# Cross attention, self-attention and mixture of experts on one core: where the self-attention weights are dequantised, and in what order the v projection stands

## Chip, cores, metric

The kernel runs on one core of one Trainium2 chip. The metric is the device time of one execution in microseconds (us), the median of several runs. A profiled execution gives a trace; its span runs from the first to the last instruction.

## What is computed

Three blocks, each added to its input: a cross attention of 128 query rows over 12544 context rows, a self-attention over the 128 rows, and a routed feed-forward block of 32 experts with one shared block. Cut to what matters here:

```
x = x + cross_attention(layernorm(x), context)       # 16 heads of 32; 257 image rows and 12287 text rows apart
x = x + self_attention(layernorm(x))                 # 16 heads of 128
x = x + moe(layernorm(x))

def mxfp4_matmul(x, codes, scales, block_size=32):
    w = codes * repeat(scales, block_size, axis=0)
    return x @ w
# in self_attention, D = 512, feat = 2048
q = mxfp4_matmul(x, wq_codes, wq_scales) + bq        # codes 512x2048, scales 16x2048; k and v alike
attn = softmax(q k^T / sqrt(128))
return mxfp4_matmul(attn v, wo_codes, wo_scales) + bo    # codes 2048x512, scales 64x512
```

Codes and scales are float32. One scale holds for 32 rows of codes, so a tile of 128 rows of codes takes 4 rows of scales, each repeated over 32 partitions. Multiplying codes by repeated scales is called dequantising below.

## The kernel before

The program is written engine by engine: each engine has its own instruction list in the order of the code, and semaphores (the names that begin with e_) say what an instruction waits for. SP issues every DMA, all on one queue. Nothing is scheduled by a planner.

**The key loop.** The context is worked through in 25 groups of 512 keys (NG = 25), each in 4 tiles of 128 (GT = 4). `steps` runs steps s = 0 to 26; step s projects group s (k and v), takes the scores and the softmax of group s - 1, and finishes group s - 2. A step goes over 16 heads; in each, TensorE does one product of queries with the stacked keys (L947), six products of a projection (L916), four transposes of softmax rows (L908) and, every fourth head, the 32 products with v (L1011). VectorE takes the row maximum (L730), folds it into the running maximum with a one-column operation between SBUF tensors (L732), and copies the transposed rows (L739). ScalarE takes the exponential (L559). GpSimd splits each context tile into a high and a low part (L470 `cx_hi`, L473 `cx_lo`) and makes the norm factors of the keys (L449, L451). SP loads the next group (L305) and builds `k_stack` for the next step in two halves of 12 DMAs of 128 KB each, SBUF to SBUF (L333); the second half waits for the last `kt_lo` (L766). The first product of the next step waits for both halves. Step 25 has no projection, step 26 only finishes.

**From the key loop to the self-attention.** After step 26 the outputs are divided, projected with `wo` (L1035) and added to x (L785, this is x1); then comes a layer norm, whose last operation is L666 (`yn`).

**The self-attention before.** The codes of q, v, k and o are loaded whole (4 MB each, `load_codes`), and their scales by sixteen 1 MB items into a ring of three buffers (`load_scales`, L361, 4 DMAs an item). `dequantise` (L285) multiplies 128x2048 elements of codes by one item, in place: the four of q and the first two of v on GpSimd behind its key loop, the other ten on VectorE between other work. TensorE projects q, v, then k (L1052, 16 products of 128x512 each), transposes the heads of q between v and k and those of k behind k (L908), takes the scores (L1073), transposes the softmax (L908), multiplies by v (L1085) and projects with the codes of o (L1090, 16 products). An item is loaded only when the buffer that it takes has been used up (`ring_free`).

**The experts.** 34 expert slices of 1.5 MB each follow through 8 slots; the first eight are released by the projections of the self-attention (`e_pj`).

## Time and profile before

| | |
|---|---|
| median of 3 runs (lowest, highest) | 1351.44 us (1350.98, 1356.18) |
| time of the profiled execution | 1353.21 us |
| its span | 1351.4 us |
| TensorE busy | 1258.6 us (93%) |
| VectorE busy | 997.9 us (74%) |
| ScalarE, GpSimd busy | 716.8 us (53%), 342.8 us (25%) |
| mean granted TensorE clock | 0.972 |

The profiled execution's time is 1.8 us over its span and 1.8 us over the median. A row of the timeline gives start, duration (both in us from the span's start; of several merged instructions the time from the first start to the last end), engine, line, operation, output<-inputs, how many, and in brackets the idle time before it with what ended it.

### The profile page before, as it was taken

The numbers are of one execution on the slowest core, as the hardware profiler recorded it, in microseconds if no ns is written. First come the engines' busy times: TensorE is split into PE (matmuls) and PEld (weight loads), VectorE is DVE, ScalarE is ACT, GpSimd is POOL, SyncE is SP. The second block draws the span as 40 slices with busy tenths as digits, with TensorE's granted clock in tenths as the row PEclk, the third lists the DMA queues.
The fourth block names the chain that finished last, engine by engine and source line by source line (L and its number), as shares of the span: only waits on it lengthen the run. The fifth ranks groups of instructions, "written<-read, shape, count | busy, mean of one in ns | idle before, by whom it ended". The sixth has DMA issues, their size and how long they took to land.

```text
span 1351.4 us, 26518 instructions
## 1 busy us (share of the span) xinstructions
PE 1258.6 (93%) x9046; PEld 998.6 (74%) x9046; DVE 997.9 (74%) x1761; ACT 716.8 (53%) x1580; POOL 342.8 (25%) x435
## 2 busy tenths in 40 slices
PE   5799999999999999999999999999998576789998
PEld 3588888888888888888888888888886332568886
DVE  3667777777777777777777777777778733659998
ACT  3646555555555555555555555555554100447776
POOL 4433222333222333222332222332221430000000
PEclk9899999999999999999999999999999687889999
DMA  7554333554333454333444333444339999969991
GB/s 272 125 157 95 95 99 89 124 124 93 91 100 89 124 124 93 88 100 92 124 124 93 85 100 94 124 120 97 83 69 268 272 271 279 312 236 368 368 358 58
DMA packets 128181, 205.34 MB, mean 152 GB/s; under 512 B 12688, under 2 KB 90512, under 8 KB 124688
## 3 DMA queue, kind: packets, MB, share of 16 engines
q1 hardware_dynamic: 128144, 204.86, 53.8%
q8 instruction: 21, 0.34, 0.1%
q14 instruction: 16, 0.13, 0.0%
HBM read 125.91 MB, written 0.26 MB: 93 GB/s over the span
## 4 chain that ended last, share of the span: by engine, by line
PE 56%; DVE 14%; issue 12%; ACT 7%; POOL 5%; DMA 4%; SPq 1%; ACTq 0%; DVEq 0%; POOLq 0%
PE ps L916 24%; PE ps L908 9%; PE ps L947 5%; DVE small L730 5%; PE ps L1011 5%; DMA scale_ring<-wk_scales 3%; ACT kt_hi L572 3%; POOL small L451 2%; DVE kb L746 2%; PE ps L1113 2%; PE ps L1116 2%; PE ps L1119 2%; DVE small L732 2%; DMA scale_ring<-wo_scales 1%; PE ps L1134 1%
## 5 line engine op out<-in xcount | busy, mean ns | idle before, releaser
L559 ACT ACTIVATE p<-ps,small 128x512 f32<-128x512 f32 (+2 forms) x400 | 271.8, 679 | 387.0 <-DVE small L732 376.7
L739 DVE COPY pt<-ps 128x512 f32<-128x512 f32 x400 | 276.0, 690 | 96.5 <-PE ps L908 95.2
L730 DVE TENSOR_REDUCE small<-ps 128x1 f32<-128x512 f32 (+2 forms) x400 | 268.3, 671 | 16.2 <-PE ps L947 16.1
L908 PE MATMUL ps<-ident,p 128*128 128x128 f32 x1600 | 241.3, 273 | 6.9 <-ACT p L559 6.9
L908 PEld LDWEIGHTS ps<-ident,p 128*128 128x128 f32 x1600 | 199.9, 140 | 59.6 <-ACT p L559 7.6
L947 PE MATMUL ps<-k_stack,q_stack 96*128 96x512 f32 x400 | 194.8, 488 | 18.3 <-ACT p L559 18.2
L470 POOL TENSOR_TENSOR cx_hi<-cx,small 128x512 fp32r<-128x512 f32 x100 | 104.6, 1046 | 215.7 <-PE ps L916 211.1
L916 PE MATMUL ps<-w_hi_k,cx_hi 128*128 128x512 f32 x384 | 151.8, 395 | 5.0 <-ACT v_sb L581 5.0
L766 DVE TENSOR_TENSOR kt_lo<-ps,kt_hi 128x512 fp32r<-128x512 f32 x100 | 69.2, 692 | 116.7 <-ACT kt_hi L572 116.7
L916 PE MATMUL ps<-w_lo_k,cx_hi 128*128 128x512 f32 x384 | 151.4, 394 | 0.0
L916 PE MATMUL ps<-w_hi_k,cx_lo 128*128 128x512 f32 x384 | 151.3, 394 | 0.0
L916 PE MATMUL ps<-w_hi_v,cx_lo 128*128 128x512 f32 x384 | 151.2, 394 | 0.0
L916 PE MATMUL ps<-w_hi_v,cx_hi 128*128 128x512 f32 x384 | 151.0, 393 | 0.0
L916 PE MATMUL ps<-w_lo_v,cx_hi 128*128 128x512 f32 x384 | 150.8, 393 | 0.0
L449 POOL TENSOR_TENSOR small<-small 128x1 f32<-128x1 f32 x100 | 19.2, 192 | 457.3 <-ACT squares L548 457.3
L473 POOL TENSOR_TENSOR cx_lo<-cx,cx_hi 128x512 fp32r<-128x512 f32 x100 | 130.9, 1309 | 7.8
L732 DVE TENSOR_TENSOR small<-small 128x1 f32<-128x1 f32 x400 | 117.5, 294 | 13.8
L947 PEld LDWEIGHTS ps<-k_stack,q_stack 96*128 96x128 f32 x400 | 76.0, 190 | 46.6 <-ACT p L559 27.4
L1011 PE MATMUL ps<-pt,v_sb 128*32 128x128 f32 x3200 | 108.9, 277 | 0.8 <-DVE pt L739 0.8
L1011 PEld LDWEIGHTS ps<-pt,v_sb 128*32 128x32 f32 x3200 | 81.8, 110 | 17.8 <-issue 16.5
L548 ACT ACTIVATE squares<-kb 128x512 f32<-128x512 f32 x100 | 63.1, 631 | 59.2 <-DVE kb L746 59.1
L829 DVE TENSOR_TENSOR w_lo<-expert,w_hi 128x2048 fp32r<-128x2048 f32 x34 | 77.8, 2292 | 10.5 <-ACT w_hi L622 10.5
(195 smaller groups left out, 1952.2 us busy)
## 6 DMA issues: line engine op xcount, KB each, us to landing
expert<-experts SPq DMA_DIRECT2D x34, 1536.0 KB, 8.9
k_stack<-kt_hi SPq DMA_DIRECT2D x400, 128.0 KB, 2.3
k_stack<-kt_lo SPq DMA_DIRECT2D x200, 128.0 KB, 2.3
cx<-ctx_t SPq DMA_DIRECT2D x24, 1024.0 KB, 5.0
codes_q<-wq_codes SPq DMA_DIRECT2D x2, 2048.0 KB, 13.6
scale_ring<-wq_scales SPq DMA_DIRECT2D x16, 256.0 KB, 20.7
codes_v<-wv_codes SPq DMA_DIRECT2D x1, 4096.0 KB, 37.6
scale_ring<-wv_scales SPq DMA_DIRECT2D x16, 256.0 KB, 14.1
```

Source lines behind the costliest of these rows:

```text
L470: eng.tensor_tensor(cx_hi[:, :, part], cx[:, :, part], one_col.unsqueeze(2).broadcast_to((P, DC, P)), ALU.mult).then_inc(e_chi, 1)
L473: eng.tensor_tensor(cx_lo[:, :, part], cx[:, :, part], cx_hi[:, :, part].bitcast(F32), ALU.subtract).then_inc(e_clo, 1)
L559: eng.activation(pb[:, lo:hi], ps_s[h % NS][:, lo:hi], exp, bias=nm[1 - par][:, h:h + 1], accum_out=ls[1 - par][:, h:h + 1]).then_inc(e_ex ...
L730: eng.tensor_reduce(ngm[:, h:h + 1], ps_s[h % NS][:, lo:hi], AX.X, ALU.max, negate=True).then_inc(e_gm, 1)
L732: eng.tensor_tensor(nm[1 - par][:, h:h + 1], ngm[:, h:h + 1], old[:, h:h + 1], ALU.min).then_inc(e_nm, 1)
L739: eng.tensor_copy(pt_sb[hp % NPT][:, :], ps_pt[hp % 2][:, :]).then_inc(e_pte, 1)
L766: eng.tensor_tensor(kt_lo[:, :, part], ps_t[:, :].rearrange("p (c k) -> p c k", c=DC), kt_hi[:, :, part].bitcast(F32), ALU.subtract).then_ ...
L829: eng.tensor_tensor(w13_lo[n % 2][:, :, :], slot[n % NR][:, 0:DC, :], w13_hi[n % 2][:, :, :].bitcast(F32), ALU.subtract).then_inc(e_13lo, 1)
L908: last = eng.transpose(dst[:, c * P:(c + 1) * P], src[:, c * P:(c + 1) * P], ident[:, :])
L916: last = eng.matmul(dst, *steps[k], start=(k == 0), stop=(k == len(steps) - 1))
L947: eng.matmul(ps_s[h % NS][:, :], q_st[qi][0:NST * HD, h, :], stk[1 - par][0:NST * HD, h, :], start=True, stop=True).then_inc(e_qk, 1)
L1011: last = eng.matmul(ps_o[jp * HD:(jp + 1) * HD, c * P:(c + 1) * P], vb[:, k, head * HD:(head + 1) * HD], pt_sb[head % NPT][:, k * P:(k + 1 ...
```

## The change

- Codes and scales are laid out on the host as 64 tiles of 128x512 (16 of each matrix). In steps 2 to 23 of the key loop, three tiles a step, SP loads a tile of codes (256 KB) and its scales (4 DMAs of 64 KB in SBUF) into one of two small buffers, GpSimd multiplies them (`scale_codes`, a 128x512 operation), and SP stores the product to a scratch tensor `scaled` in HBM (`pass_codes`).
- After the key loop the four matrices are loaded whole from `scaled` (`load_matrix`, 4 MB each). Nothing is dequantised behind the key loop any more, on GpSimd or VectorE. The q and k biases and `bo` are asked for at other places of the queue: `bo` directly behind the matrix o.
- The order of the projections is q, k, v. The transposes of q stand between the blocks of k; three of the four blocks of v stand behind the scores, among the transposes of the softmax. The product with o waits for each quarter of its input apart.
- VectorE adds the four v biases between the steps of its softmax, and adds `bo` to x1 before the first of them.
- Buffers are placed anew; `wo` is loaded behind the key loop instead of in step 1.

The diff, cut to its core (a line of ... marks what is left out):

```diff
-        QKV = "qvk"
-        codes = {n: sb(f"codes_{n}", off * KB, [P, DC, SF]) for n, off in (("q", 0), ("v", 64), ("k", 32))}
-        codes_o = sb("codes_o", 96 * KB, [P, SH, D])
-        NRING = 3
-        ring = [sb(f"scale_ring{i}", (144 + 8 * i) * KB, [P, SF]) for i in range(NRING)]
...
+        QKV = "qkv"
+        NWT = SH
+        NW = 4 * NWT
+        W_STEP, W_FIRST = 3, 2
+        codes = [sb(f"codes{i}", (96 + 4 * i) * KB, [P, D]) for i in range(2)]
+        code_scale = [sb(f"code_scale{i}", (98 + 4 * i) * KB, [P, D]) for i in range(2)]
...
-        def dequantise(eng, n, c, done):
-
-            eng.wait_ge(e_codes[n], 16 * (c // (DC // 2) + 1 if n == "q" else 1))
-            scale = ring_loaded(eng, scales(n, c))[:, :]
-            part = codes_o[:, c * HB:(c + 1) * HB, :] if n == "o" else codes[n][:, c, :]
-            if n == "o":
-                scale = scale.rearrange("p (c f) -> p c f", c=HB)
-            eng.tensor_tensor(part, part, scale, ALU.mult).then_inc(done, 1)
...
+        scaled = nc.dram_tensor("scaled", (NW, P, D), F32, kind="Internal").ap()
+
+        def tile_of(array, i):
+            return array[i:i + 1] if isinstance(i, int) else array[bass.ds(i, 1)]
...
@@ -315,12 +296,33 @@
             load_weight(2)
             load_weight(3)
 
+            def pass_codes(s, k, par, loop):
+
+                i = s * W_STEP + (k - W_FIRST * W_STEP)
+                if not loop and not 0 <= i <= NW:
+                    return
+                b = (par + k) % 2
+                if loop or i >= 1:
+                    eng.wait_ge(e_cm, i)
+                    eng.dma_start(tile_of(scaled, i - 1).rearrange("o p f -> p (o f)"), codes[1 - b][:, :]).then_inc(e_cs[1 - b], 16)
+                if not loop and i == NW:
+                    return
+                if loop or i >= 2:
+                    eng.wait_ge(e_cs[b], i * 8 - 8 * b)
+                eng.dma_start(codes[b][:, :], tile_of(t["codes"], i).rearrange("o p f -> p (o f)")).then_inc(e_cl[b], 16)
+                for r in range(P // QB):
+                    eng.dma_start(code_scale[b][r * QB:(r + 1) * QB, :],
+                                  tile_of(t["code_scales"], i)[:, r, :].partition_broadcast(QB)).then_inc(e_cl[b], 16)
+
...
                     eng.wait_ge(e_clo, s * GT + GT)
                     load(s + 1)
+                if not loop and s == W_FIRST:
+                    eng.wait_ge(e_qk, NH)
+                pass_codes(s, 0, par, loop)
                 if not loop and s == 1:
                     eng.wait_ge(e_vp, GT)
...
                         for j in range(HC):
                             eng.dma_start(stk[par][r * HD:(r + 1) * HD, j::HC, keys].bitcast(F32),
                                                      part[j * HD:(j + 1) * HD, :, keys].bitcast(F32)).then_inc(e_stk, 16)
-                if not loop and s == 1:
-                    eng.wait_ge(e_qk, NH)
-                    eng.dma_start(wo[:, :, :], wview(t["o_wt"])).then_inc(e_wo, 16)
+                    pass_codes(s, 1 + half, par, loop)
 
...
+            def load_matrix(n):
+
+                i = (QKV + "o").index(n) * NWT
+                eng.dma_start(weight[n][:, :, :], scaled[i:i + NWT].rearrange("i p f -> p i f")).then_inc(e_wl[n], 16)
 
...
-            eng.wait_ge(e_kp, NG * GT)
-            load_codes("q", 0)
-            eng.wait_ge(e_clo, NG * GT)
-            load_scales("q", 0)
+            for b in range(2):
+                eng.wait_ge(e_cs[b], 16 * (NW // 2))
+            eng.wait_ge(e_vp, NG * GT)
+            load_matrix("q")
+            eng.dma_start(wo[:, :, :], wview(t["o_wt"])).then_inc(e_wo, 16)
             eng.wait_ge(e_stk, (16 * HALVES * NST * HC) * NG)
             for i, n in enumerate(["o_b", "v_b", "v_img_b"]):
...
+            load_bias("q")
+            load_bias("k")
             eng.wait_ge(e_qk, (NG - 1) * NH)
-            load_codes("v")
-            load_scales("q", 3)
-            load_scales("v", 0)
-            load_scales("v", 1)
-            eng.wait_ge(e_pv, NG * NH // HC)
-            load_bias("q")
-            load_scales("v", 2)
-            load_scales("v", 3)
+            load_matrix("k")
+            eng.wait_ge(e_pv, (NG - 1) * (NH // HC))
             load_bias("v")
             eng.wait_ge(e_qk, NG * NH)
-            load_codes("k")
+            load_matrix("v")
             eng.wait_ge(e_x1, 1)
-            for c in range(DC):
-                load_scales("k", c)
-            load_bias("k")
-            load_codes("o")
-            for c in range(NB):
-                load_scales("o", c)
+            load_matrix("o")
...
@@ -449,6 +421,14 @@
                 eng.tensor_tensor(k_t[:, j:j + 1], k_ss[:, j:j + 1], rms_eps, ALU.add).then_inc(e_rt, 1)
                 eng.wait_ge(e_rt, s * GT + j + 1)
                 eng.tensor_tensor(k_r[:, j:j + 1], k_t[:, j:j + 1], minus_half, ALU.pow).then_inc(e_r, 1)
...
+            def scale_codes(i, b, loop):
+
+                if not loop and not 0 <= i < NW:
+                    return
+                n = 16 * (1 + P // QB)
+                eng.wait_ge(e_cl[b], i * (n // 2) + (n - b * n // 2))
+                eng.tensor_tensor(codes[b][:, :], codes[b][:, :], code_scale[b][:, :], ALU.mult).then_inc(e_cm, 1)
...
+                    if j % 2 == 1:
+                        k = (j + 1) // 2
+                        scale_codes(s * W_STEP + (k - (W_FIRST + 1) * W_STEP), (1 - par + k) % 2, loop)
...
+                scale_codes(s * W_STEP - W_FIRST * W_STEP, par, loop)
...
-            steps(eng, step)
-            for c in range(DC):
-                dequantise(eng, "q", c, e_deqp)
+            steps(eng, step, peeled=1)
             eng.wait_ge(e_var, 2)
             rsqrt(rstd, mv[:, 1:2], ln_eps)
-            for c in range(NPOOL - DC):
-                dequantise(eng, "v", c, e_deqp)
...
-            for b in range(NB):
-                add_bias("q", b)
-                if b < NB - 1 and NPOOL - DC + b < DC:
-                    dequantise(eng, "v", NPOOL - DC + b, e_deq)
-            for b in range(NB):
-                add_bias("v", b)
-                dequantise(eng, "k", b, e_deq)
-            for b in range(NB):
-                add_bias("k", b)
-            for c in range(NB // 2):
-                dequantise(eng, "o", c, e_deq)
+            for n in "qk":
+                for b in range(NB):
+                    add_bias(n, b)
+            eng.wait_ge(e_bo, 16)
+            chain(eng.tensor_tensor(x1[:, :], x1[:, :], bo_row[:, :], ALU.add))
+            add_bias("v", 0)
             for b in range(NB):
...
                 eng.tensor_scalar(s_nb[:, hs], s_max[:, hs], -SD ** -0.5, None, ALU.mult).then_inc(e_smax, 1)
             for b in range(NB):
+                if b < NB - 1:
+                    add_bias("v", b + 1)
...
-            for c in range(NB // 2, NB):
-                dequantise(eng, "o", c, e_deq)
-            eng.wait_ge(e_bo, 16)
-            chain(eng.tensor_tensor(x1[:, :], x1[:, :], bo_row[:, :], ALU.add))
...
-            project("q")
-            project("v")
-            transpose_heads("q", 0)
-            project("k")
-            transpose_heads("k", NB)
-            eng.wait_ge(e_trc, 2 * NB)
-            for b in range(NB):
...
+            def project(n, b):
+                i = QKV.index(n) * NB + b
+                if b == 0:
+                    eng.wait_ge(e_wl[n], 16)
+                if i >= 2:
+                    eng.wait_ge(e_pjb, i - 1)
+                for c in range(DC):
+                    last = eng.matmul(ps_pj[b % 2][:, :], ynt[:, c * P:(c + 1) * P], weight[n][:, c * NB + b, :],
+                                      start=(c == 0), stop=(c == DC - 1))
+                last.then_inc(e_pj, 1)
+
...
-            for b in range(NB + 1):
-                if b < NB:
-                    eng.wait_ge(e_sn, b + 1)
-                    if b >= 2:
...
+            def weigh_values(b):
+                eng.wait_ge(e_sptc, b + 1)
+                eng.wait_ge(e_pjb, 2 * NB + b + 1)
+                for h in range(b * HB, (b + 1) * HB):
+                    part = slice(h * P, (h + 1) * P)
+                    last = eng.matmul(ps_sc[b][:, (h % HB) * P:(h % HB + 1) * P], sv[:, part], spt[:, part], start=True, stop=True)
+                last.then_inc(e_so, 1)
...
+            for b in range(NB):
+                project("q", b)
+            for b in range(NB):
+                project("k", b)
+                transpose_heads("q", b)
+            for b in range(NB - 1):
+                transpose_heads("k", b)
+            project("v", 0)
+            transpose_heads("k", NB - 1)
+            for b in range(NB):
+                scores(b)
+            project("v", 1)
+            project("v", 2)
+            transpose_p(0)
+            project("v", 3)
+            transpose_p(1)
+            for b in range(NB):
+                weigh_values(b)
+                if b + 2 < NB:
+                    transpose_p(b + 2)
+            eng.wait_ge(e_wl["o"], 16)
             for h in range(SH):
-                last = eng.matmul(ps_pj[0][:, :], sot[:, h * P:(h + 1) * P], codes_o[:, h, :], start=(h == 0), stop=(h == SH - 1))
+                if h % HB == 0:
+                    eng.wait_ge(e_soc, h // HB + 1)
+                last = eng.matmul(ps_pj[0][:, :], sot[:, h * P:(h + 1) * P], weight["o"][:, h, :], start=(h == 0), stop=(h == SH - 1))
             last.then_inc(e_sf, 1)
```

Three places of the program follow, on SP, GpSimd and TensorE; the names in them are the tiles, with buffer numbers.

SP, step 2 of the key loop, between the two halves of `k_stack` (the later steps are alike, with register instructions for the addresses); before:

```order
L333 DMA k_stack_63<-kt_hi 32x4x256 x4
L333 DMA k_stack_63<-kt_hi 32x4x256 [waits kt_lo]
L333 DMA k_stack_63<-kt_hi 32x4x256 x3
L333 DMA k_stack_63<-kt_lo 32x4x256 x4
L333 DMA k_stack_63<-kt_hi 32x4x256 x4
```

and now:

```order
L335 DMA k_stack_63<-kt_hi 32x4x256 x4
L307 DMA scaled<-codes_104 128x512 [waits codes_scaled]
L312 DMA codes_105<-codes 128x512
L314 DMA code_scale_107<-code_scales 32x512 x4
L335 DMA k_stack_63<-kt_hi 32x4x256 [waits kt_lo]
L335 DMA k_stack_63<-kt_hi 32x4x256 x3
L335 DMA k_stack_63<-kt_lo 32x4x256 x4
```

Six DMAs now stand between the halves. Another six stand behind the second half, and six behind the load of the context.

GpSimd, in the loop, around the second context tile of a step; before:

```order
L470 TENSOR_TENSOR cx_hi<-cx,small 128x4x128 [waits v_projected]
L472 REGISTER_ALU
L473 TENSOR_TENSOR cx_lo<-cx,cx_hi 128x4x128 [waits cx_hi]
L469 REGISTER_ALU
L470 TENSOR_TENSOR cx_hi<-cx,small 128x4x128 [waits v_projected]
```

and now:

```order
L450 TENSOR_TENSOR cx_hi<-cx,small 128x4x128 [waits v_projected]
L452 REGISTER_ALU
L453 TENSOR_TENSOR cx_lo<-cx,cx_hi 128x4x128 [waits cx_hi]
L430 ISA
L431 TENSOR_TENSOR codes_105<-codes_105,code_scale_107 128x512 [waits codes_loaded1]
L449 REGISTER_ALU
L450 TENSOR_TENSOR cx_hi<-cx,small 128x4x128 [waits v_projected]
```

A multiplication of codes stands behind the second split; a second one stands behind the fourth, a third behind the last norm factor.

TensorE, self-attention, from the scores on; before:

```order
L1073 MATMUL ps<-skt,sqt 128x128 [waits self_transposed_stored]
L1073 MATMUL ps<-skt,sqt 128x128 x15
L908 MATMUL ps<-ident,sq 128x128 [waits self_normed]
L908 MATMUL ps<-ident,sq 128x128 x3
L908 MATMUL ps<-ident,sq 128x128 [waits self_normed]
L908 MATMUL ps<-ident,sq 128x128 x3
L1085 MATMUL ps<-sk,sv 128x128 [waits self_p_stored]
```

and now, from the last quarter of the scores on:

```order
L1038 MATMUL ps<-skt,sqt 128x128 x3
L1022 MATMUL ps<-weight_v,ynt 128x512 [waits self_biased]
L1022 MATMUL ps<-weight_v,ynt 128x512 x3
L1022 MATMUL ps<-weight_v,ynt 128x512 [waits self_biased]
L1022 MATMUL ps<-weight_v,ynt 128x512 x3
L880 MATMUL ps<-ident,sq 128x128 [waits self_normed]
L880 MATMUL ps<-ident,sq 128x128 x3
L1022 MATMUL ps<-weight_v,ynt 128x512 [waits self_biased]
L1022 MATMUL ps<-weight_v,ynt 128x512 x3
L880 MATMUL ps<-ident,sq 128x128 [waits self_normed]
L880 MATMUL ps<-ident,sq 128x128 x3
L1052 MATMUL ps<-sk,sv 128x128 [waits self_biased,self_p_stored]
```

Three blocks of the v projection (four products each) moved to between the scores and the products with v.

## Rows read from the trace of the kernel before

**Rows 1.** Page, the chain that ended last, share of the span by engine

```profile
PE 56%; DVE 14%; issue 12%; ACT 7%; POOL 5%; DMA 4%; SPq 1%; ACTq 0%; DVEq 0%; POOLq 0%
```

**Rows 2.** Stretches: length, busy (count) of PE, PEld, DVE, ACT, POOL; clock, DMA share, GB/s

```profile
240.00:1000.00 760.00, 751.35 (x6065) 615.22 (x6064) 581.83 (x1142) 421.65 (x1008) 231.75 (x300) 1.00 0.41 103
1028.15:1063.85 35.70, 21.48 (x220) 15.44 (x216) 34.18 (x54) 12.88 (x33) 13.54 (x3) 0.87 1.02 328
1089.24:1190.55 101.31, 78.83 (x240) 41.96 (x240) 42.03 (x41) 18.21 (x50) 2.85 (x5) 0.87 1.02 303
1196.84:1350.00 153.16, 150.23 (x681) 122.17 (x681) 141.71 (x159) 113.75 (x136) 0.00 (x0) 0.99 0.72 269
```

**Rows 3.** Timeline of VectorE in step 25

```profile
1037.39 0.16 DVE L732 TENSOR_TENSOR small<-small 128x1 f32<-128x1 f32 x1
...
1038.79 4.25 DVE L732 TENSOR_TENSOR small<-small 128x1 f32<-128x1 f32 x1
...
1055.09 3.55 DVE L732 TENSOR_TENSOR small<-small 128x1 f32<-128x1 f32 x1
...
1059.87 3.36 DVE L732 TENSOR_TENSOR small<-small 128x1 f32<-128x1 f32 x1
```

**Rows 4.** Timeline of GpSimd in step 25

```profile
1038.52 4.51 POOL L285 TENSOR_TENSOR codes_q<-codes_q,scale_ring 128x2048 f32<-128x2048 f32 x1 [27.20 <-DMA scale_ring<-wq_scales]
```

**Rows 5.** Timeline of VectorE: last operation of the second and third layer norm

```profile
1082.68 4.71 DVE L666 TENSOR_SCALAR yn<-x,small 128x512 f32<-128x512 f32 x1 [0.94 <-POOL small L444]
...
1193.17 0.55 DVE L666 TENSOR_SCALAR x<-x,small 128x512 f32<-128x512 f32 x1 [0.94 <-POOL small L444]
```

**Rows 6.** Timeline of TensorE in the self-attention (two records a product)

```profile
1089.24 15.43 PE L1052 MATMUL ps<-codes_q,ynt 128*128 128x512 f32 x32 [0.69 <-ACT ynt L596]
1104.51 10.46 PE L1052 MATMUL ps<-codes_v,ynt 128*128 128x512 f32 x24
1124.50 6.27 PE L1052 MATMUL ps<-codes_v,ynt 128*128 128x512 f32 x8 [9.53 <-DVE sv L796]
1130.61 1.04 PE L908 MATMUL ps<-ident,sq 128*128 128x128 f32 x8
...
1155.11 3.84 PE L1073 MATMUL ps<-skt,sqt 128*128 128x128 f32 x32 [0.69 <-ACT skt L600]
1165.45 1.97 PE L908 MATMUL ps<-ident,sq 128*128 128x128 f32 x8 [6.50 <-DVE sq L820]
...
1173.76 2.10 PE L1085 MATMUL ps<-sk,sv 128*128 128x128 f32 x16
1176.55 14.00 PE L1090 MATMUL ps<-codes_o,skt 128*128 128x512 f32 x32 [0.69 <-ACT skt L614]
```

**Rows 7.** Timeline of SP in one step of the loop, second half of the stack

```profile
525.36 7.89 SPq L333 DMA_DIRECT2D k_stack<-kt_hi  x8
...
535.89 2.54 SPq L333 DMA_DIRECT2D k_stack<-kt_hi  x4
```

**Rows 8.** Tile k_stack, 240 to 1000 us: from the start of an issue to landing

```profile
DMA to landing us min/median/max: 2.3/2.3/2.5
```

**Rows 9.** Timeline of TensorE: first product of two successive steps

```profile
500.65 0.50 PE L947 MATMUL ps<-k_stack,q_stack 96*128 96x512 f32 x1
...
541.29 0.50 PE L947 MATMUL ps<-k_stack,q_stack 96*128 96x512 f32 x1
```

**Rows 10.** Timeline of VectorE in that step

```profile
530.00 0.69 DVE L766 TENSOR_TENSOR kt_lo<-ps,kt_hi 128x512 fp32r<-128x512 f32 x1 [0.72 <-ACT kt_hi L572]
...
531.32 1.22 DVE L732 TENSOR_TENSOR small<-small 128x1 f32<-128x1 f32 x1
```

**Rows 11.** Tile scale_ring: issue time on SP in ns, min/median/max

```profile
L361 SPq DMA_DIRECT2D scale_ring<-wq_scales x16: 310/422/588, 1026.2 to 1044.5; - x16
```

**Rows 12.** Stretches: a context load; loads of repeated scale rows

```profile
545.00:546.00 1.00, 1.00 (x9) 0.84 (x7) 0.49 (x3) 0.66 (x2) 0.00 (x0) 1.00 1.01 393
1146.00:1158.00 12.00, 10.97 (x56) 7.06 (x55) 3.71 (x4) 2.17 (x4) 0.00 (x0) 1.00 1.07 218
```

119 lines of the change are left out of this document (38 added, 81 removed).

## The prediction

> **What bounds the kernel now.** I read the chain that ended last first: it lies on TensorE for 56% of the span, and on nearly every other engine for a part [rows 1], so I went on to the stretches, to see where each counts. In the key loop TensorE is busy 751.35 of 760 us at full clock [rows 2]: it is the bound there, and everything else has room (GpSimd works 231.75 us of it). A step takes 541.29 - 500.65 = 40.6 us [rows 9], so TensorE idles (760 - 751.35) / (760 / 40.6) = 0.46 us a step. With the experts TensorE is again busy 150.23 of 153.16 us. Between them lie two stretches of another kind: in step 25 VectorE is busy 34.18 of 35.70 us and TensorE only 21.48, and in the 101.31 us of the self-attention TensorE has 78.83 us of work, part of it at half clock (0.87 on average against 1.00 in the loop), while the DMA share is 1.02 [rows 2]. So the loop and the experts can only be disturbed by this change; what can be won lies between 1028 and 1190 us.
>
> **Part 1, GpSimd's multiplications leave step 25.** The running maximum, L732, takes 0.16 us on VectorE, but three of them in step 25 take 4.25, 3.55 and 3.36 us [rows 3]. The first begins inside one of GpSimd's multiplications of codes and ends with it: 1038.52 + 4.51 = 1043.03, and 1038.79 + 4.25 = 1043.04 [rows 3, 4]; the other two fall on the next two multiplications. Everything behind waits, since the exponential needs this maximum. Without the multiplications 4.25 + 3.55 + 3.36 - 3 x 0.16 = 10.7 us go. Nothing else sits on GpSimd there in the new program, so the term can't be less than about 10; I see no row that would make it more.
>
> The Trainium skill has a rule for this (SBUF — State Buffer, section "SBUF: two separate sides"): VectorE and GpSimd share one pair of SBUF ports, and an operation of VectorE with two SBUF inputs is blocked for the whole of a GpSimd operation that reads SBUF. The trace agrees. The rule speaks against this change as well, since 64 new multiplications enter the loop: if each held up the path for its whole length, 64 x 1.13 = 72 us would be lost, and the kernel would be slower. I weigh that in part 4 by rows.
>
> **Part 2, the layer norm.** L666, which makes `yn`, takes 4.71 us, and the same operation in the next layer norm 0.55 [rows 5]; the first ran beside the multiplications of v's codes. They go: 4.71 - 0.55 = 4.2 us.
>
> **Part 3, the self-attention.** Its length before is 101.3 us (1089.24 to 1190.55). TensorE idled 9.53 us in front of v's last block (behind scales) and 6.50 in front of the first transposed softmax [rows 6]. Now no multiplication stands in the way, if the matrices are there (below), and the list of TensorE is: q's 16 products 15.4 us as now, the low clock at their start included; k and v at the rate of the 12 products in 10.46 us, 0.87 each, 32 x 0.87 = 27.9; eight head transposes at 1.04 / 2 = 4.2; scores 3.8; four softmax transposes 2.1; 16 products with v at 2.10 / 8 = 4.2; o 14.0 [rows 6]. The sum is 71.6. The wait of 6.50 is covered by two blocks of v (7.0 us); if it were not, it would come back. For waits that stay I add 1.4, two handoffs of 0.69. So 73.0 instead of 101.3: 28.3 us less. Upwards this term is bounded by the 6.5 us of softmax latency, downwards by the 1.4.
>
> **The loads behind the loop.** They start when the last projection ends, about 1028. Four matrices, `wo` and x are 18.1 MB; rows of context, also 2 KB each, come at 393 GB/s, repeated rows at 218 [rows 12]. 18.1 / 0.393 = 46 us, plus 4.2 MB of repeated biases at 218 GB/s = 19 us: the last one, `bo`, lands near 1093. The self-attention would start at 1089.24 - 14.9 = 1074.3; k is wanted 15 us, v 33 us later, o later still. `bo` is the tight one: VectorE waits for it before the maxima of the scores. With two blocks of v as cover it costs something from about 1074.3 + 37 = 1111 on. So the loads are hidden, by some 18 us.
>
> **Part 4, what the loop pays.** Three tiles a step for 22 steps.
> SP: the second half of the stack is released by `kt_lo` at 530.00 + 0.69 = 530.7 [rows 10]. The first half's twelfth issue ends at 525.36 + 4 x 0.635 = 527.9, taking 2.54 / 4 = 0.635 for one [rows 7]. In these 2.8 us SP must now issue six DMAs. The nearest rows are the scale loads, also plain two-dimensional patterns: 0.42 [rows 11], with the gap 0.46 each, 2.8 us; register instructions add a little. At the price of a stack DMA it is 3.8 us. So the second half starts 0 to 1.2 us late. Its last issue starts at 535.89 + 3 x 0.635 = 537.8 and lands 2.3 us later, 540.1 [rows 7, 8]; the product that needs it starts at 541.29 [rows 9], so the slack is 1.2 us: the whole range is just covered, and I take nothing.
> GpSimd: 4.51 / 4 = 1.13 us a tile [rows 4], 3.4 a step, on an engine that idles 70% of it. The splits are wanted by TensorE a good part of a step later.
> VectorE: each multiplication can hold an L732 as the split does now (1.22 instead of 0.16, [rows 10]). Below it is nothing, if they fall where no L732 is due. Above, the three splits that collide now leave TensorE idle 0.46 us a step, and three more would double that: 22 x 0.46 = 10 us. I take 0.1 a step, 2.2 us, near the lower end, because a held L732 is mostly absorbed: the exponential waited for is two heads ahead of its need.
> The experts: their list is unchanged, and TensorE bounds it. The first slots are asked for behind q's projection, far ahead of use. Nothing.
>
> **The sum.** -10.7 - 4.2 - 28.3 + 2.2 = -41.0 us on a span of 1351.4: 1310.4. The profiled execution's time is 1353.2, so 1312.2 for it; the median of the runs is 1.8 below that, so 1310.4 again for the median.
>
> **Rivals.**
> The forecast, 1310, own range 1302 to 1318: chance 0.62.
> The loop pays more: SP's issues cost over 0.635 us or register instructions add half a microsecond, and the stack lands late, or the held L732s add up. For it: the slack is 1.2 us against a lag of up to 1.2. Against it: the 0.42 us of [rows 11]. It decides once the second half starts over 1.2 us late, or each multiplication meets an L732; at 0.46 to 1.0 us a step the time is 1308.2 + 10 to 22, 1318 to 1330. Chance 0.22.
> The loads are late: all of them at the 218 GB/s of the repeated rows, 22.3 / 0.218 = 102 us, `bo` lands at 1130, 19 us after it is wanted: 1329. For it: the share of the engines is over 1 in this stretch. Against it: the matrices have no repeated rows. It decides below 18.1 / (1111 - 1028 - 19) = 283 GB/s. Chance 0.08.
> The self-attention doesn't get denser: TensorE's granted clock stays at 1.2 GHz for much of it, as in v's last block, where four products took 6.27 us instead of 3.5 [rows 6]. That comes after an idle time, and the new list has no long one. All 48 behind q at 1.57 instead of 0.87 would give back 34 us: 1344. Chance 0.04.
> Slower: GpSimd's list is in order. If a multiplication waits for its codes, the norm factors and splits behind it wait too; the norm factors lead to `kt_lo`, and that to the stack and the next step. From 43.2 / 22 = 2.0 us a step the gain is gone, from 2.3 the kernel is measurably slower; at 3 us a step it is 1308.2 + 66 = 1374. Against it: a tile is asked for some 13 us before the one after it, and a DMA of half its size lands in 2.3 us [rows 8]. Chance 0.04.
>
> The Trainium skill's rule for such loads (DMA: Bandwidth & Descriptors, section "Rules for kernel authors") is to make them 1 MiB or more, as below 64 KB one pays mostly overhead; the scale loads are 64 KB each. By it the three passes of a step would be slow; whether that is seen depends on the slack above, not on the rule.
>
> **Range and chances.** The likeliest case gives 1310. To leave out no more than 2 in 10 the range runs from 1301 to 1330: it takes in the forecast's own range and most of the second and third case. A measurement of this kernel tells 0.5% from no change, 6.8 us. Faster by more: the first three cases and a part of the rest, 0.93; within it 0.03; slower 0.04.
>
> **What the profile after would show.** Step 25 without an L732 over 1.3 us, and about 11 us shorter. `yn` in 0.55 us. From the first q product to the end of o some 73 us, with no idle time of TensorE over 1 us and its clock near 1. In the loop a step of 40.6 to 40.8 us; a step of over 41.1 says that the loop pays, and then the wait in front of L947 (behind the stack) or the lengths of L732 tell which way. The prediction is wrong if the stack becomes what the first product of a step waits for, if VectorE waits for `bo`, or if GpSimd waits long for codes.

## The result, and the profile after

| | before | after |
|---|---|---|
| median (lowest, highest) of 4 runs | 1351.21 us (1350.66, 1356.18) | 1312.02 us (1310.86, 1313.31) |
| time of the profiled execution, its span | 1353.21, 1351.4 us | 1312.13, 1310.4 us |
| ratio of after to before, 95% interval | | 0.9702 [0.9678, 0.9727] |

The predicted time was 1310.4 us. The spans of the two profiled executions differ by 41.0 us, which is the predicted sum to the tenth, and the medians by 39.2; the stages do not agree that well. For the stages I take the starts of single instructions in both traces: ScalarE's exponential of the step of the maxima, which ends a step's softmax (L588 before, L568 after), the addition that makes x1, the first product of q, the last of o, and the first expert product. One of the six executions of experiment 8's kernel below took 2078.06 us at a granted clock of 0.557 and is left out of its median.

| stage | before | after | difference | predicted |
|---|---|---|---|---|
| start to the end of step 1 | 94.16 | 94.66 | +0.5 | 0 |
| end of step 1 to the end of step 24 | 933.90 | 937.95 | +4.1 | +2.2 |
| to the end of step 25 | 35.89 | 26.15 | -9.7 | -10.7 |
| to x1 | 16.16 | 15.46 | -0.7 | 0 |
| x1 to the first product of q | 9.13 | 4.57 | -4.6 | -4.2 |
| first product of q to the end of o | 101.31 | 70.55 | -30.8 | -28.3 |
| to the first expert product | 6.29 | 5.93 | -0.4 | 0 |
| to the end | 154.56 | 155.15 | +0.6 | 0 |

The stretches of the changed kernel that answer to [rows 2] (length, busy time of PE, PEld, DVE, ACT, POOL, clock, DMA share, GB/s): the loop, step 25, the self-attention, the experts.

```profile
240.00:1000.00 760.00, 749.35 (x6029) 613.78 (x6028) 609.03 (x1137) 419.99 (x1004) 300.28 (x355) 1.00 0.59 160
1032.71:1058.76 26.05, 20.87 (x220) 15.14 (x216) 23.72 (x54) 12.96 (x34) 0.00 (x0) 0.93 1.01 380
1078.79:1149.34 70.55, 69.87 (x240) 36.97 (x240) 19.94 (x31) 18.51 (x50) 0.00 (x0) 0.98 0.64 245
1155.27:1310.00 154.73, 150.83 (x681) 122.75 (x681) 141.77 (x159) 113.88 (x136) 0.00 (x0) 0.98 0.72 267
```

In the self-attention TensorE is now busy 69.87 of 70.55 us at a clock of 0.98, against 78.83 of 101.31 at 0.87. In step 25 VectorE has 23.72 us of work instead of 34.18: the same 54 operations, and GpSimd none. The loop is the stage that got worse: VectorE 609 us busy for 582, with fewer operations.

TensorE in the self-attention, which answers to [rows 6]:

```profile
1078.79 15.70 PE L1022 MATMUL ps<-weight_q,ynt 128*128 128x512 f32 x32 [0.69 <-ACT ynt L576]
...
1111.70 3.60 PE L1022 MATMUL ps<-weight_v,ynt 128*128 128x512 f32 x8
1115.14 0.60 PE L880 MATMUL ps<-ident,sk 128*128 128x128 f32 x4
1115.58 3.74 PE L1038 MATMUL ps<-skt,sqt 128*128 128x128 f32 x32
1119.15 7.03 PE L1022 MATMUL ps<-weight_v,ynt 128*128 128x512 f32 x16
1126.02 0.60 PE L880 MATMUL ps<-ident,sq 128*128 128x128 f32 x4
...
1131.72 0.66 PE L880 MATMUL ps<-ident,sq 128*128 128x128 f32 x4 [0.33 <-DVE sq L796]
...
1135.44 13.90 PE L1079 MATMUL ps<-weight_o,skt 128*128 128x512 f32 x32
```

The two blocks of v (7.03 us) stand where the wait of 6.50 us was, and the softmax is there when they end. VectorE in the layer norm and at `bo`, which answers to [rows 5]:

```profile
1076.79 0.59 DVE L645 TENSOR_SCALAR yn<-x,small 128x512 f32<-128x512 f32 x1 [0.93 <-POOL small L416]
...
1109.64 0.69 DVE L775 TENSOR_TENSOR sk<-ps,sk 128x512 f32<-128x512 f32 x1 [3.18 <-PE ps L1022]
1110.25 0.68 DVE L781 TENSOR_TENSOR x<-x,bo_row 128x512 f32<-128x512 f32 x1
```

There is no bracket at L781: `bo` had landed. In step 25 each of the sixteen running maxima (L711 now, L732 before) takes 0.16 us, such as

```profile
1039.14 0.16 DVE L711 TENSOR_TENSOR small<-small 128x1 f32<-128x1 f32 x1
```

**Where the loop lost 4 us.** From the first product of queries of step 2 to that of step 5, and from there to that of step 24, the two kernels need 121.99 and 772.00 us before, 123.92 and 774.13 after: half of the loss lies in three steps, half in the other nineteen. The waits of TensorE between 240 and 1000 us (line, what it waited for, us in total, times, longest), first before, then after:

```profile
PE ps L947 <- ACT p L559: 8.7, 19, 0.5
```

```profile
PE ps L919 <- ACT p L539: 10.7, 19, 0.9
```

So the steady loop doesn't wait for the stack, but once a step for `p`, as it did before, only longer. The wait is always at the same place, 27.0 us into the step, in front of the product of head 11, which needs the exponential of head 9. VectorE, GpSimd and TensorE of the changed kernel there, in the step that begins at 503.71 and lasts 40.98 us (one of the longer ones; the mean of steps 5 to 23 is 40.74):

```profile
528.94 0.68 DVE L709 TENSOR_REDUCE small<-ps 128x1 f32<-128x512 f32 x1
529.65 1.02 DVE L711 TENSOR_TENSOR small<-small 128x1 f32<-128x1 f32 x1
530.60 0.68 DVE L718 COPY pt<-ps 128x512 f32<-128x512 f32 x1
```

```profile
526.51 0.55 POOL L423 TENSOR_TENSOR small<-small 128x1 f32<-128x1 f32 x1
527.02 1.28 POOL L431 TENSOR_TENSOR codes<-codes,code_scale 128x512 f32<-128x512 f32 x1
528.27 1.03 POOL L450 TENSOR_TENSOR cx_hi<-cx,small 128x512 fp32r<-128x512 f32 x1
529.39 1.28 POOL L453 TENSOR_TENSOR cx_lo<-cx,cx_hi 128x512 fp32r<-128x512 f32 x1
```

```profile
531.54 0.50 PE L919 MATMUL ps<-k_stack,q_stack 96*128 96x512 f32 x1 [0.80 <-ACT p L539]
```

It is not the multiplication that holds the running maximum, but the low part of the split, which runs from 529.39 to 530.67; L711 ends at 530.67 with it. The multiplication is over by 528.30, and what it does is to stand in front of the split in GpSimd's list: the high part begins 24.56 us into this step, and 24.20 us into the step of the kernel before that begins at 500.65. There the low part holds the maximum of head 9 as well, with a wait of 0.46 us of TensorE behind it:

```profile
525.97 1.28 POOL L473 TENSOR_TENSOR cx_lo<-cx,cx_hi 128x512 fp32r<-128x512 f32 x1
526.31 0.96 DVE L732 TENSOR_TENSOR small<-small 128x1 f32<-128x1 f32 x1
528.13 0.50 PE L947 MATMUL ps<-k_stack,q_stack 96*128 96x512 f32 x1 [0.46 <-ACT p L559]
```

SP in the same step of the changed kernel:

```profile
528.73 2.56 SPq L335 DMA_DIRECT2D k_stack<-kt_hi  x4
531.46 0.46 SPq L307 DMA_DIRECT2D scaled<-codes  x1
532.20 0.36 SPq L312 DMA_DIRECT2D codes<-codes  x1
532.74 1.84 SPq L314 DMA_DIRECT2D code_scale<-code_scales  x4
534.63 2.54 SPq L335 DMA_DIRECT2D k_stack<-kt_hi  x4
...
539.81 2.56 SPq L335 DMA_DIRECT2D k_stack<-kt_hi  x4
```

The halves are 3.3 us apart; the last issue ends at 539.81 + 2.56 = 542.37, the next step's first product starts at 544.69, 2.3 us later.

### The profile page after: what moved, and what is told of

It is laid out like the page before. It is cut to its first block, busy times and chain, and to the rows that moved or that the text cites. A ratio compares the mean times of both kernels' runs of the same rounds, so it can differ in the third digit from the quotient of the medians.

```text
span 1310.4 us, 27717 instructions
## 1 busy us (share of the span) xinstructions
PE 1248.2 (95%) x9046; PEld 993.7 (76%) x9046; DVE 995.3 (76%) x1751; ACT 716.8 (55%) x1580; POOL 394.9 (30%) x493
## 4 chain that ended last, share of the span: by engine, by line
PE 59%; DVE 13%; issue 11%; ACT 6%; POOL 4%; SPq 4%; DMA 1%; DVEq 0%; ACTq 0%; POOLq 0%
PE ps L888 23%; PE ps L880 9%; PE ps L919 5%; DVE small L709 5%; PE ps L983 5%; PE ps L1022 3%; SPq L335 3%; PE ps L1102 2%; PE ps L1105 2%; PE ps L1108 2%; ACT kt_hi L552 2%; DVE kb L725 2%; POOL small L423 2%; DVE small L711 2%; PE ps L1123 1%
## 5 line engine op out<-in xcount | busy, mean ns | idle before, releaser
L718 DVE COPY pt<-ps 128x512 f32<-128x512 f32 x400 | 275.6, 689 | 67.9 <-PE ps L880 66.2
L709 DVE TENSOR_REDUCE small<-ps 128x1 f32<-128x512 f32 (+2 forms) x400 | 268.2, 670 | 14.0 <-PE ps L919 13.9
L711 DVE TENSOR_TENSOR small<-small 128x1 f32<-128x1 f32 x400 | 139.5, 349 | 13.8
L431 POOL TENSOR_TENSOR codes<-codes,code_scale 128x512 f32<-128x512 f32 x64 | 82.2, 1285 | 68.3 <-DMA code_scale<-code_scales 68.3
```

What stands on the lines that cost most here:

```text
L431: eng.tensor_tensor(codes[b][:, :], codes[b][:, :], code_scale[b][:, :], ALU.mult).then_inc(e_cm, 1)
L709: eng.tensor_reduce(ngm[:, h:h + 1], ps_s[h % NS][:, lo:hi], AX.X, ALU.max, negate=True).then_inc(e_gm, 1)
L711: eng.tensor_tensor(nm[1 - par][:, h:h + 1], ngm[:, h:h + 1], old[:, h:h + 1], ALU.min).then_inc(e_nm, 1)
L718: eng.tensor_copy(pt_sb[hp % NPT][:, :], ps_pt[hp % 2][:, :]).then_inc(e_pte, 1)
```

## Experiments

Two theories stood against each other for the loop: **SP** (six issues between the halves of the stack) and **GpSimd** (its multiplications, by whatever they hold or push). Two points outside the loop were tested as well: the hold of VectorE in step 25, and v's place. The table gives for every kernel the median, its ratio to the kernel before on the same chip, and the lengths of steps 2 to 4 and 5 to 23 (differences of the starts of first products, in us).

| kernel | median us (n) | ratio [95%] | steps 2-4 | steps 5-23 |
|---|---|---|---|---|
| before | 1351.21 (4) | | 121.99 | 772.00 |
| after | 1312.02 (4) | 0.9702 [0.9678, 0.9727] | 123.92 | 774.13 |
| after, run again | 1311.92 (5) | 0.9693 [0.9674, 0.9712] | 123.74 | 773.63 |
| 1 no pass | 1309.42 (5) | 0.9680 [0.9658, 0.9701] | 122.02 | 772.17 |
| 2 one column | 1309.57 (5) | 0.9686 [0.9666, 0.9707] | 123.78 | 772.14 |
| 3 pass ahead | 1308.28 (5) | 0.9675 [0.9652, 0.9699] | 122.46 | 772.16 |
| 4 v before k | 1320.12 (5) | 0.9756 [0.9734, 0.9778] | 125.04 | 773.74 |
| 5 GpSimd held | 1350.96 (1) | | 122.00 | 772.02 |
| 6 put back | 1331.50 (4) | 0.9844 [0.9828, 0.9861] | 124.32 | 774.52 |
| 7 twice | 1313.02 (4) | 0.9711 [0.9693, 0.9728] | 125.94 | 773.51 |
| 8 multiply ahead | 1310.61 (5) | 0.9687 [0.9667, 0.9707] | 124.30 | 772.27 |
| 9 pass ahead, low part waits | 1291.62 (5) | 0.9542 [0.9523, 0.9560] | 120.55 | 758.21 |
| 10 low part waits only | 1312.70 (5) | 0.9685 [0.9661, 0.9708] | 127.93 | 772.19 |
| 11 before, low part waits | 1336.84 (4) | 0.9882 [0.9849, 0.9915] | 119.95 | 758.21 |

The intervals of 1, 2, 3, 8 and of the changed kernel overlap; between these the step lengths of the traces decide, one trace each. In the four traces with the loop of the changed kernel (itself twice, 4 and 6) steps 2 to 4 take 123.7 to 125.0 us and steps 5 to 23 take 773.6 to 774.5; smaller differences say nothing.

**1, the price of the pass.** `pass_codes` and `scale_codes` return at once, the loads behind the loop no longer wait for them, and the matrices are loaded from the codes themselves, so that the weights stay unscaled. Of the diff, the line in `load_matrix`:

```diff
-                eng.dma_start(weight[n][:, :, :], scaled[i:i + NWT].rearrange("i p f -> p i f")).then_inc(e_wl[n], 16)
+                eng.dma_start(weight[n][:, :, :], t["codes"][i:i + NWT].rearrange("i p f -> p i f")).then_inc(e_wl[n], 16)
```

> This kernel is the changed one without the pass over the weight tiles in the key loop; the four weights are loaded from the codes themselves, so the output lacks the scaling. Theory: the pass is what made the loop up to the end of step 24 4.6 us longer than before; the step falls back to 40.63 us and the time to 1307 to 1308.5 us. Rival: the longer loop comes from the placing of buffers or from the loads behind it, and the time stays at 1311.5 to 1312.5.

The loop from the end of step 1 to that of step 24 takes 934.47 us, 3.5 less than 937.95 and 0.6 more than before, and every step from 3 to 21 takes 40.63 to 40.65 (22 and 23 take 40.69). The pass is the loop's loss. The median came out 1 us above the expected: other stages vary by as much, such as step 25, 26.7 us here at a clock of 0.94.

**2, the multiplication without its length.** Loads, stores and waits stay; all columns of a tile but the first are left unscaled.

```diff
-                eng.tensor_tensor(codes[b][:, :], codes[b][:, :], code_scale[b][:, :], ALU.mult).then_inc(e_cm, 1)
+                eng.tensor_tensor(codes[b][:, 0:1], codes[b][:, 0:1], code_scale[b][:, 0:1], ALU.mult).then_inc(e_cm, 1)
```

> The changed kernel with GpSimd's multiplication of a tile cut to its first column; loads, stores and waits stay, the weights are left unscaled but for 1 column in 512. Theory SP: what the loop pays is the 3.3 us of code issues that stand on SP between the halves of the key stack; it stays at 40.65 to 40.75 us a step and the time at 1311 to 1312.5. Rival GpSimd: what the loop pays is the multiplication (GpSimd's list, VectorE held by it); the time falls to 1307.5 to 1309.

Each theory has half: steps 5 to 23 fall to 772.14, steps 2 to 4 stay at 123.78. In the steady loop it was GpSimd and not SP, against my theory. The median, 1309.57, lies between the two expected ranges, 0.6 us over that of GpSimd.

**3, SP's pass ahead of the stack, and with it the multiplication.**

```diff
                 pass_codes(s, 0, par, loop)
+                pass_codes(s, 1, par, loop)
...
-                    pass_codes(s, 1 + half, par, loop)
+                pass_codes(s, 2, par, loop)
...
                     key_norm(s, j)
-                scale_codes(s * W_STEP - W_FIRST * W_STEP, par, loop)
+                    if j == 1:
+                        scale_codes(s * W_STEP - W_FIRST * W_STEP, par, loop)
```

> The changed kernel with the second piece of a step's code pass moved from between the halves of the key stack to ahead of the first half (SP is idle there for 11.6 us), and GpSimd's multiplication for it two key norms earlier. Theory SP: the second half of the stack waits for its keys again and not for SP; steps of 40.63 us, 1308 to 1309.5 us in all. Rival GpSimd: the multiplications are all still there, 1311.5 to 1312.5. Third: the multiplication held back a key norm at the new place, over 1314.

The time came out as theory SP had it, but not for its reason alone: the edit moves both. Steps 2 to 4 fall by 1.5 us, of which only step 4 keeps 0.5, and steps 5 to 23 by 2.0, with all multiplications still there. That called for the two parts singly.

**8, the multiplication ahead, SP as it was.** The edit is the last piece of the diff above alone.

> The changed kernel with only GpSimd's multiplication of the first tile of a step done two key norms earlier; SP's order stays, its code pass between the halves of the stack too. Theory now (GpSimd's list): the multiplication stood at 23.3 us into the step, just ahead of the split of the context, pushed the low part of it by up to 0.5 us over VectorE's running maximum and so p; with it gone from there the steps from the 5th on are 40.63 us and the wait is 0.45 us again, while steps 2 to 4 keep their waits for the stack (41.0 to 41.6): loop to the end of step 24 935.5 to 936.5 us, 1309.5 to 1311 in all. Rival (SP's pass between the halves): loop 937.5 to 938.5, 1312 to 1313.

Steps 5 to 23 take 772.27 and TensorE's wait for `p` is again 8.7 us in 19, steps 2 to 4 stay long at 124.30: as the theory had it (loop 936.48), the rival's 937.5 is not reached. The median, 1310.61, is in the expected range. The multiplications still hold running maxima here. All running maxima that start between 240 and 1000 us (count, busy us, mean ns, idle before), in the changed kernel and in this one:

```profile
L711 DVE TENSOR_TENSOR small<-small 128x1 f32<-128x1 f32 x298 | 111.6, 375 | 10.3
```

```profile
L712 DVE TENSOR_TENSOR small<-small 128x1 f32<-128x1 f32 x299 | 116.0, 388 | 10.3
```

The kernel before has 83.6 us of them. So 32 us more of running maxima cost the steady steps of this kernel 0.3 us (772.27 for 772.00): nearly all of these holds are absorbed, and what counts is when the low part beside head 9 begins.

**7, every multiplication twice.** The scales are so applied twice.

```diff
+                eng.tensor_tensor(codes[b][:, :], codes[b][:, :], code_scale[b][:, :], ALU.mult).then_inc(e_c1, 1)
+                eng.wait_ge(e_c1, i + 1)
                 eng.tensor_tensor(codes[b][:, :], codes[b][:, :], code_scale[b][:, :], ALU.mult).then_inc(e_cm, 1)
```

> The changed kernel with every multiplication of a code tile done twice (the scaling is so applied twice). Theory SP: the second lies in the slack of SP's waits for it; 1311.5 to 1313.5 us. Rival GpSimd: each multiplication costs the loop by itself, so the price of the loop, 4.1 us, comes once more or more than once; 1315.5 to 1325.

64 more multiplications cost steps 5 to 23 nothing (773.51), and steps 2 to 4, at 125.94, 1 to 2 us. So the price is not so much for each multiplication, but goes by where they stand.

**9, the low part waits for the maximum.** If the split holds the running maximum of head 9, the split should come after it. On top of experiment 3:

```diff
                     eng.wait_ge(e_chi, s * GT + j + 1)
+                    if j <= 1 and (loop or s >= 2):
+                        eng.wait_ge(e_nm, s * NH + (10 + 2 * j - 2 * NH))
                     eng.tensor_tensor(cx_lo[:, :, part], cx[:, :, part], cx_hi[:, :, part].bitcast(F32),
                                                  ALU.subtract).then_inc(e_clo, 1)
```

> The kernel with the pass ahead of the first half, and besides it the low part of the context split (tiles 0 and 1 of each) held until VectorE has the running maximum of head 9 (11). Theory: the wait for p at 27.0 us into the step is the low part's hold of VectorE (running maximum 0.96 us in place of 0.16); it goes, the step becomes 40.18 to 40.25 us, 21 steps give 8 to 9.5 us: 1299 to 1301.5 us. Rival: the maximum of head 9 is late for another reason, or another wait (the key stack, last issue to first product 2.85 us, shortest seen 1.95) takes its place: 1307 to 1309.5.

A step is 39.91 us, and the kernel 20.3 us faster than the changed one on the same chip. The same place on VectorE and GpSimd, then the stretch of the loop:

```profile
519.16 0.68 DVE L713 TENSOR_REDUCE small<-ps 128x1 f32<-128x512 f32 x1
519.88 0.16 DVE L715 TENSOR_TENSOR small<-small 128x1 f32<-128x1 f32 x1
519.95 0.69 DVE L722 COPY pt<-ps 128x512 f32<-128x512 f32 x1
```

```profile
520.11 1.29 POOL L456 TENSOR_TENSOR cx_lo<-cx,cx_hi 128x512 fp32r<-128x512 f32 x1 [0.66 <-DVE small L715]
```

```profile
240.00:1000.00 760.00, 760.00 (x6170) 626.14 (x6169) 562.43 (x1163) 430.98 (x1029) 300.81 (x358) 1.00 0.59 159
```

GpSimd now waits 0.66 us, the maximum takes 0.16, and TensorE is busy 760 of 760 us. The gain was larger than I expected: 0.72 us a step for a wait of 0.45 us in the trace. Matmul ends are modelled, so that a wait can be longer than its row; I leave it at that. The number itself stood in the first trace: in step 24 the context is used up and no split stands beside heads 9 and 11, and it takes 39.91 us in the kernel before and in the changed one too, where step 23 takes 40.63 and 40.69.

**10, the same wait without the pass ahead,** on the changed kernel, for tile 0 only:

> The changed kernel with its multiplications and SP's order as they are, and only the low part of tile 0 held until the running maximum of head 9. Theory: the whole wait for p goes, 0.45 us a step and the multiplication's share of it; but SP's pass between the halves leaves the stack 0.3 us above its shortest way (2.3 us against 1.95), so that about 0.35 us a step come: steps of 40.2 to 40.4, 1303 to 1307 us. Rival (the hold is not by the low part): 1311.5 to 1313.

Wrong on both sides: the time is the rival's (the five go from 1306.76 to 1313.47), but not for its reason, since the wait for `p` is gone. Steps 5 to 23 are 1.9 us shorter than in the changed kernel, no more than moving the multiplication alone gave, and steps 2 to 4 are 3 to 4 us longer. The waits of TensorE between 240 and 1000 us:

```profile
PE ps L921 <- DMA k_stack<-kt_hi: 8.4, 18, 0.6
```

The stack has taken its place. VectorE's last `kt_lo` of the step that begins at 507.53, and SP:

```profile
536.29 0.69 DVE L747 TENSOR_TENSOR kt_lo<-ps,kt_hi 128x512 fp32r<-128x512 f32 x1 [0.73 <-ACT kt_hi L554]
```

```profile
536.49 1.84 SPq L314 DMA_DIRECT2D code_scale<-code_scales  x4
538.37 2.54 SPq L335 DMA_DIRECT2D k_stack<-kt_hi  x4
```

The keys are there at 536.98, and the second half begins at 538.37, when the issues before it are done; in experiment 9 it begins at once, 29.3 us into the step. With the held maximum out of the way, SP's six issues between the halves set the step, to 772.19 / 19 = 40.64 us on average. So two limits lay almost on each other: experiment 3 lifts that of SP and leaves that of the split (772.16), this one lifts that of the split and leaves that of SP (772.19), experiment 9 lifts both (758.21). What the wait of tile 1, which is in 9 and not here, gives by itself was not tested.

**11, the wait in the kernel before.** The edit of experiment 9's diff alone.

> The kernel before the change with only the low part of tiles 0 and 1 of the context split held until the running maximum of head 9 (11). If the 17 us of the kernel that has this wait and the pass ahead of the stack are the split's hold of VectorE alone, which has stood in the kernel before as well: steps of 39.91 us, loop to the end of step 24 918 us in place of 933.9, 1334 to 1337.5 us in all. Rival (they need the changed kernel's code): above 1345.

Steps of 39.91 us, the loop 918.64, 1336.84 us, against a median of 1352.52 us of the kernel before on the same chip. The hold was in the kernel before all along and has nothing to do with the change. Step 25 and the self-attention stay within 1.5 us of what they were.

**4, v's place.** In TensorE's list the four blocks of v go between q and k, its biases on VectorE likewise:

```diff
+            for b in range(NB):
+                project("v", b)
             for b in range(NB):
                 project("k", b)
...
-            project("v", 1)
-            project("v", 2)
             transpose_p(0)
-            project("v", 3)
             transpose_p(1)
```

> The changed kernel with the v projection put back ahead of the k projection on TensorE and VectorE; all else stays. Theory: the move of v covers the softmax, in which TensorE waited 6.5 us before; 1317.5 to 1319.5 us. Rival: the multiplications beside the softmax were what made that wait, and without them v's place matters little; 1312 to 1314.5.

From the first q product to the first of o 63.41 us against 56.65: v's place is worth 6.8 us. The wait before the first softmax transpose is only 1.80 us, though, where it was 6.50 [rows 6]:

```profile
1129.00 3.74 PE L1035 MATMUL ps<-skt,sqt 128*128 128x128 f32 x32
1134.53 0.66 PE L877 MATMUL ps<-ident,sq 128*128 128x128 f32 x4 [1.80 <-DVE sq L793]
...
1137.33 2.07 PE L1049 MATMUL ps<-sk,sv 128*128 128x128 f32 x8 [1.33 <-ACT sk L589]
```

Further waits of 0.16 and 1.33 us stand behind it; the products with v and the softmax transposes among them take up the rest. The expected 6.5 us was right in size, and its place half wrong; the median is 0.6 us over the expected range, with a loop of 939.23 us.

**5, GpSimd held in the kernel before.**

```diff
+            eng.wait_ge(e_osum, 1)
             for c in range(DC):
                 dequantise(eng, "q", c, e_deqp)
```

> The kernel before the change with GpSimd's multiplications of q and v held until the attention output is summed, so that none stands beside step 25. Only the stage from the end of step 24 to the end of step 25 is read: theory (GpSimd's long multiplications hold VectorE) 25 to 27 us in place of 35.9, and the held multiplications with p, of 3.4 to 4.3 us, gone. Rival (the step is long for its own work or for the loads beside it): 35 to 36. The time in all says little, since q's four multiplications of 4.5 us now stand behind the sum: 1345 to 1362.

Step 25 takes 25.24 us in place of 35.89, 10.65 less. The multiplications stand later now; one of v's meets the layer norm:

```profile
1080.81 4.71 DVE L667 TENSOR_SCALAR yn<-x,small 128x512 f32<-128x512 f32 x1 [8.78 <-POOL small L444]
```

and the first product of q waits for q's (16.98 us from x1, 9.13 before), so that the whole is 1350.96 in its one execution, against a median of 1353.16 of the kernel before on the same chip.

**6, put back.** The changed kernel with five multiplications on GpSimd that nothing needs, of 128x2048. The diff is cut: the load of the matrix o waits for the fourth of them, and the first bias of the projections for the fifth.

```diff
             steps(eng, step, peeled=1)
+            eng.wait_ge(e_wl["q"], 16)
+            eng.wait_ge(e_bias["q"], 16)
+            for i in range(4):
+                eng.wait_ge(e_un, i)
+                eng.tensor_tensor(unused[0][:, :], weight["q"][:, 0:4, :].rearrange("p i f -> p (i f)"), sq[:, :], ALU.mult).then_inc(e_un, 1)
             eng.wait_ge(e_var, 2)
             rsqrt(rstd, mv[:, 1:2], ln_eps)
+            eng.tensor_tensor(unused[1][:, :], weight["q"][:, 0:4, :].rearrange("p i f -> p (i f)"), sq[:, :], ALU.mult).then_inc(e_un, 1)
```

> The changed kernel with five GpSimd multiplications of 128x2048 that nothing needs: four beside step 25, one beside the layer norm. Theory: step 25 grows from 26.2 us by 7 to 10 and the layer norm's last operation from 0.59 to between 2 and 4.7; 1320 to 1326 us. Rival: what shortened step 25 was another order of loads; it stays within 1 us of 26.2, 1312 to 1314 us.

VectorE and GpSimd:

```profile
1056.48 3.60 DVE L720 TENSOR_TENSOR small<-small 128x1 f32<-128x1 f32 x1
...
1070.38 3.47 DVE L740 TENSOR_TENSOR small<-small 128x16 f32<-128x16 f32 x1
...
1091.31 4.85 DVE L654 TENSOR_SCALAR yn<-x,small 128x512 f32<-128x512 f32 x1 [0.94 <-POOL small L419]
```

```profile
1055.55 18.27 POOL L476 TENSOR_TENSOR unused<-weight_q,sq 128x2048 f32<-128x2048 f32 x4 [38.76 <-issue]
...
1091.24 4.50 POOL L479 TENSOR_TENSOR unused<-weight_q,sq 128x2048 f32<-128x2048 f32 x1
```

Step 25 grows to 35.76 us, the way to x1 from 15.46 to 19.44 (L740 of step 26 is held too), the way to q's first product from 4.57 to 9.29: +18.3 us, and 19.5 in the median. That is more than expected: four long multiplications back to back reach into step 26. The mechanism is the one expected, and both terms, step 25 and the layer norm, can so be put back.

## Why the prediction was right, point by point

**Part 1, step 25: right.** 10.7 us predicted. The changed kernel's profiled execution shows 9.7, a second one of the same kernel 10.66 (25.23 us), and the held GpSimd of experiment 5 10.65. The difference goes with the granted clock of the step: 0.93 in the first of these, 1.00 in the others. The traces of experiments 1 to 4 and 7 to 10 agree: 25.2 us at a clock of 1.00, 26.7 at 0.94. The Trainium skill's rule that the prediction cites (SBUF — State Buffer, section "SBUF: two separate sides") holds in the rows above: an L711 that starts during a GpSimd operation ends with it, while L709 and L718, which read PSUM, run on beside it (none of them takes over 0.70 us between 240 and 1000 us).

**Part 2, the layer norm: right.** 4.2 us predicted, 4.6 measured; `yn` takes 0.59 us, and 4.85 with the multiplication put back.

**Part 3, the self-attention: right in kind, 2.5 us too small.** The list of TensorE was costed from rows with the waits of the old kernel in them. The head transposes come every 0.43 us instead of 1.04 / 2, a block of v or k every 3.44 instead of 3.49, and the 1.4 us of waits added for safety are 0.7 behind the start. Of the 30.8 us, 6.8 are v's place (experiment 4); the other 24 came with the multiplications gone and the new order of the transposes, which I didn't take apart.

**The loads: right.** `bo` landed at 1092.8, where 1093 was predicted; its addition at 1110.25 waits for nothing, and no product of TensorE waits for a matrix. In the loop GpSimd does wait for the scales of its tiles, 55.4 us in 36 waits between 240 and 1000 us, the longest 2.6 us; TensorE waits for no split behind it.

**Part 4, what the loop pays: half of the real size, and the reason was wrong.** +2.2 was predicted for steps 2 to 23, and +4.1 came, 3.5 of which go with the pass. It has two parts.

In steps 5 to 23 the loss was 2.1 us (1.6 in the second execution), 0.11 a step, where 0.1 was predicted. That this size fits is luck, since the way there was another. The prediction let a multiplication hold a running maximum, and rightly took this as mostly absorbed. What it ruled out was the other way: "GpSimd: 4.51 / 4 = 1.13 us a tile [rows 4], 3.4 a step, on an engine that idles 70% of it. The splits are wanted by TensorE a good part of a step later." A tile takes 1.28 us, and TensorE indeed never waits for a split; but a split pushed back by a few tenths falls otherwise onto VectorE, and the one at 27 us into the step stands on TensorE's path. I costed what the new operations hold, not what they push. The loss is gone when the multiplication has no length (experiment 2) or stands elsewhere (3, 8).

In steps 2 to 4 the loss was 1.9 us, where the SP line took nothing. The line was right for the steady loop: the six issues between the halves take 3.3 us, between the 2.8 and 3.8 of the prediction, the last issue starts near 541.8 and lands some 2.4 us later, 0.5 us before the product at 544.69 of the 1.2 us that were there, and nothing is lost. In steps 2 to 4, though, TensorE waits 0.3 to 0.5 us in front of the first product for the stack, which the prediction had named as a sign that it is wrong; the pass ahead takes away 1.5 of the 1.9 us. The six issues end 31.5, 31.1 and 31.0 us into these steps, and 30.5 to 30.6 into steps 5 to 8. Why these steps have less room than the later ones is open.

The errors cancel: +1.0 in step 25, +2.4 in the loop and its start, -2.5 in the self-attention, -0.9 over the other stages. That the difference of the spans fits to the tenth is chance.

**What the prediction read and didn't follow.** It has the 0.46 us by which TensorE idles in every step, and the 1.22 us of L732 from [rows 10] as "the split", and used both as an upper bound for the new multiplications alone. It also counts three splits a step that collide; the trace shows two maxima held, 0.96 us at 526.31 and 1.22 at 531.32, both by a low part, and a wait of TensorE behind the first alone. The pair was worth 15.7 us of the kernel before (experiment 11), for two waits in GpSimd's list.

## What to carry to other kernels

Where one operation in each round makes the bounding engine wait a few tenths of a microsecond, look for what the other engines run at that moment, and order it behind; a wait put on the engine with room (GpSimd, 0.66 us) can free the one without. When work is added to an engine that idles, cost not only what it takes and holds, but where everything behind it in that engine's list will land. And when the removal of a wait wins nothing, look whether another wait has come up at the same length before giving up the theory: here two limits had to go together.

## What the runs showed of the hardware that was not expected

A GpSimd operation between SBUF tiles that is 1.28 us long holds a one-column operation of VectorE for 0.8 to 1.1 us; the two such holds of a step cost the loop 0.72 us a step. Over 240 to 1000 us the running maximum takes, before and with experiment 9 (count, busy us, mean ns, idle before):

```profile
L732 DVE TENSOR_TENSOR small<-small 128x1 f32<-128x1 f32 x300 | 83.6, 279 | 10.4
```

```profile
L715 DVE TENSOR_TENSOR small<-small 128x1 f32<-128x1 f32 x305 | 50.7, 166 | 10.5
```

An issue on SP costs by its pattern: 0.60 us for a DMA of the stack (0.64 from start to start), 0.33 us for a scale load of 64 KB (315 to 448 ns; 0.50 from start to start). The scale loads landed in the loop after 1.9 to 3.3 us beside a context load and a stack of 3 MB. In the loop the DMA engines went from a share of 0.41 to 0.59, and a landing in the stack from 2.3 / 2.3 / 2.5 us (lowest, median, highest) to

```profile
DMA to landing us min/median/max: 2.3/2.4/2.9
```
